# Second mixture of experts: gate and up from copied weights with H1 on the partitions, and gathers unspaced from the third half on

## The reference, cut to what matters

```python
# flat: 4096 x 128; gate_w, up_w: 32 x 128 x 128; down_w: 32 x 128 x 128
scores = softmax(flat @ router_w.T + router_bias)
topk_scores, topk_idx = top_k(scores, 4)
topk_scores /= topk_scores.sum(-1)
h = silu(flat x gate_w) * (flat x up_w)          # for each token and expert
expert_out = h x down_w
out = sum over the 4 chosen of expert_out * topk_score
out += silu(flat @ sgate_w.T) * (flat @ sup_w.T) @ sdown_w.T
x = layernorm(x + out)
```

## Time and profile before

| | us |
|---|---|
| median of 3 runs (lowest to highest) | 1296.8 (1296.16 to 1298.94) |
| time of the profiled execution | 1300.21 |
| its span in the profile | 1298.4 |
| TensorE busy | 1010.7 (78%) |
| VectorE busy | 811.9 (63%) |
| ScalarE busy | 547.4 (42%) |
| GpSimd busy | 489.5 (38%) |

### The profile page before, as it was taken

How to read it: one execution, slowest core, us unless ns; L and a number is a source line. 1 busy time by engine, 2 the same in 40 slices (tenths; PEclk the granted TensorE clock), 3 DMA queues, 4 the chain that set the end, 5 groups by cost and what they waited for, 6 DMA issues and landing times. The chain is left out here.

```text
span 1298.4 us, 20321 instructions
## 1 busy us (share of the span) xinstructions
PE 1010.7 (78%) x6768; PEld 602.2 (46%) x6768; DVE 811.9 (63%) x2127; ACT 547.4 (42%) x878; POOL 489.5 (38%) x484
## 2 busy tenths in 40 slices
PE   5772119952589899989989998988788989997971
PEld 3662016741234344434434443443247878874541
DVE  3757860132677788787887878688727443555643
ACT  1341004422136556665556665464464433431241
POOL 4101145525515410352004530143435544556776
PEclk8985558986569799997999999798899999999995
DMA  4225403421322211231122312353127756641122
GB/s 114 66 65 162 74 11 92 120 63 40 103 74 55 76 33 46 47 107 40 41 60 53 101 49 78 84 142 135 46 78 209 216 165 170 174 124 39 45 76 65
DMA packets 113122, 114.88 MB, mean 88 GB/s; under 512 B 17813, under 2 KB 95253, under 8 KB 109781
## 3 DMA queue, kind: packets, MB, share of 16 engines
q1 hardware_dynamic: 73830, 74.07, 20.7%
q0 software_dynamic: 12048, 25.71, 7.2%
q10 hardware_dynamic: 27144, 13.83, 3.7%
HBM read 67.94 MB, written 41.94 MB: 85 GB/s over the span
## 5 line engine op out<-in xcount | busy, mean ns | idle before, releaser
L2158 DVE TENSOR_REDUCE maxima<-psum 128x1 f32<-128x512 f32 (+4 forms) x624 | 385.5, 643 | 109.7 <-PE psum L1973 57.3
L2096 ACT ACTIVATE probs<-psum 128x1024 f32<-128x1024 f32 (+3 forms) x384 | 299.2, 809 | 271.9 <-PE psum L1992 206.4
L2006 PE MATMUL psum<-probs,v_wide 128*32 128x512 f32 (+3 forms) x1536 | 175.9, 532 | 0.0
L1969 PE MATMUL psum<-ka,qa 75*128 75x512 bf16 (+3 forms) x440 | 145.7, 344 | 28.4 <-DVE maxima L2158 22.8
L1481 POOL DMA_INDIRECT sorted<-x_rows,to_row x76 | 75.5, 993 | 209.3 <-ACT probs L2096 114.0
L2517 ACT ACTIVATE g_silu<-psum 128x512 f32<-128x512 f32 x80 | 47.8, 598 | 177.3 <-PE psum L2423 101.0
L1988 PE MATMUL psum<-qa,ka 78*128 78x512 bf16 (+3 forms) x440 | 118.4, 334 | 4.7 <-DMA qa<-max_parts 2.4
L1407 POOL DMA_INDIRECT w_gu<-expert_out,to_row x64 | 65.4, 1022 | 136.8 <-ACT probs L2096 95.3
L1969 PEld LDWEIGHTS psum<-ka,qa 75*128 75x128 bf16 x440 | 42.9, 99 | 129.5 <-DVE maxima L2158 111.0
L2423 PE MATMUL psum<-w_gu,g_xT 128*128 x384 | 95.4, 391 | 9.1 <-DVE g_h L2593 5.4
L116 POOL DMA_INDIRECT f_got<-expert_out,dense x64 | 63.9, 998 | 68.2 <-DMA f_got<-expert_out,dense 43.7
(11 more groups left out here) (333 smaller groups left out, 1825.7 us busy)
## 6 DMA issues: line engine op xcount, KB each, us to landing
g_rows<-sorted SPq DMA_DIRECT2D x192, 64.0 KB
expert_out<-g_y ACTq DMA_DIRECT2D x48, 256.0 KB
qa<-q_steps SPq DMA_DIRECT2D x30, 192.0 KB
ka<-k_steps SPq DMA_DIRECT2D x10, 576.0 KB
w<-in_W SPq DMA_DIRECT2D x16, 256.0 KB, 3.1
w_gu<-in_gu SPq DMA_DIRECT2D x4, 1024.0 KB, 10.7
sorted<-blank SPq DMA_DIRECT2D x54, 64.0 KB
q_steps<-w_gu SPq DMA_DIRECT2D x12, 256.0 KB
```

Source lines behind the costliest of these rows:

```text
L1969: mm = pe.matmul(bank[:, h * width:h * width + plain], qa[b][0:ROWS_MAX, h0 + h, qt * P:(qt + 1) * P], ka[b][0:ROWS_MAX, h0 + h, seg * HAL ...
L2006: mm = pe.matmul(B[OUT][32 * h:32 * (h + 1), q0 - c * HALF:HALF], v_wide[s.buf][:, j, h, PAD * (1 - c):PAD * (1 - c) + 32], probs[k % PRIN ...
L2096: act.activation(probs[k % PRING][:, 2 * pair:2 * pair + 2, 0:w], PS[:, 2 * pair:2 * pair + 2, 0:w], ACT.Exp).then_inc(exps, 1)
L2158: dve.tensor_reduce(maxima[:, seg, h0:h0 + heads, qt], bank[:, 0:heads * width].rearrange("p (h k) -> p h k", h=heads), AX.X, ALU.max).the ...
```

## The change

It does five things.

1. **Gate and up.** The operands change places. The expert's weights are stationary, once the gate half and once the up half, and xT streams past, 128 columns per tile. The result has H1 on the partitions and tokens along the free dimension, gate in one PSUM bank (two in turn) and up in another. The product h is already what the down product needs, so emit_hT and copy_hT go.
2. **Weights.** ScalarE copies each group's four [gate | up] blocks (128x256) from w_gu to one of two buffers w_now, at addresses from registers; it reads the expert numbers for two groups at even n. TensorE still reads them for the down product.
3. **Order.** The down product, the output copy and the store come one group sooner (n-1, n-1, n-2). On ScalarE the weight copies of n+1 stand between the store and SiLU n.
4. **Gathers.** PACED_HALVES is 2, so halves 2 and 3 are unspaced.
5. **Sums.** Their places in the two tables move.

```diff
-PACED_HALVES = 4
-SUMS_BESIDE_GROUPS = {31: (0, 0), 35: (0, 1), 38: (1, 0), 41: (1, 1), 45: (2, 0)}
-SUMS_BESIDE_CHUNKS = {(0, 1): (2, 1), (1, 0): (3, 0), (2, 0): (3, 1), (2, 3): (4, 0),
+PACED_HALVES = 2
+SUMS_BESIDE_GROUPS = {32: (0, 0), 36: (0, 1), 40: (1, 0), 44: (1, 1)}
+SUMS_BESIDE_CHUNKS = {(0, 0): (2, 0), (0, 3): (2, 1), (1, 2): (3, 0), (2, 1): (3, 1), (3, 0): (4, 0),
...
             if m < GROUPS:
-                return GU[:, :, 0, :], GU[:, :, 1, :]
+                return B[1 + 2 * (m % 2)], B[2]
...
                 def emit_group(n):
                     pe.wait_ge(xT_done, n + 1)
-                    wait_past(pe, h_done, n)
-                    for s in range(FT):
-                        at = (s % 2) * 2 * H1
-                        mm = pe.matmul(B[1 + s // 2][:, at:at + 2 * H1], xT[n % 2][:, s * P:(s + 1) * P],
-                                       w_gu[:, bass.ds(experts[n][s] * (2 * H1), 2 * H1)], start=(s % 2 == 0), stop=True,
-                                       skip_group_check=True)
-                    mm.then_inc(gu_psum, 1)
+                    pe.wait_ge(w_copied, n + 1)
+                    for x, (bank, filled) in enumerate(zip(gate_up(n), (gate_psum, gu_psum))):
+                        if x:
+                            wait_past(pe, h_done, n)
+                        for s in range(FT):
+                            mm = pe.matmul(bank[:, s * P:(s + 1) * P], w_now[n % 2][:, s, x * H1:(x + 1) * H1],
+                                           xT[n % 2][:, s * P:(s + 1) * P], start=(s == 0), stop=True, skip_group_check=True)
+                        mm.then_inc(filled, 1)
...
                     if n in PART_ENDS:
-                        emit_y(n - 2)
-                        emit_hT(n)
                         emit_y(n - 1)
                         emit_y(n)
                     if n + 1 < GROUPS:
                         emit_xT(n + 1)
-                    if n >= 2 and not within_end(n):
-                        emit_y(n - 2)
+                    if n and not within_end(n):
+                        emit_y(n - 1)
...
+                def copy_weights(n):
+                    if n % 2 == 0:
+                        load_experts(n)
+                    wait_past(act, gu_psum, n - 1)
+                    for s in range(FT):
+                        last = act.activation(w_now[n % 2][:, s, :], w_gu[:, bass.ds(experts[n][s] * (2 * H1), 2 * H1)], ACT.Copy)
+                    last.then_inc(w_copied, 1)
...
+                act.wait_ge(G.experts_loaded, 5 * 16)
+                copy_weights(0)
                 copy_xT(0)
                 for n in range(GROUPS):
-                    if n >= 3 and n - 3 not in range(PART_GROUPS - 3, PART_GROUPS):
-                        store(n - 3)
+                    if n >= 2 and n - 2 not in range(PART_GROUPS - 2, PART_GROUPS):
+                        store(n - 2)
                     if n == 1:
                         emit_scale(act, S, 1, LAST, x_last, 0, TB // 2)
+                    if n + 1 < GROUPS and n not in PART_ENDS:
+                        copy_weights(n + 1)
                     emit_silu(n)
-                    if n and n - 1 not in PART_ENDS:
-                        copy_hT(n - 1)
                     if n in PART_ENDS:
-                        copy_hT(n)
-                        for m in range(n - 2, n + 1):
+                        for m in range(n - 1, n + 1):
                             store(m)
                     if n == EXP_AT:
                         emit_exp1(act, S, LAST)
+                    if n in PART_ENDS:
+                        copy_weights(n + 1)
                     if n + 1 < GROUPS:
                         copy_xT(n + 1)
...
                 def emit_h(n):
-                    split = lambda x: x[:].rearrange("p (s h) -> p s h", s=FT)
+                    dve.wait_ge(gu_psum, n + 1)
                     dve.wait_ge(silu_done, n + 1)
-                    wait_past(dve, hT_psum, n - 1)
-                    dve.tensor_tensor(split(h[n % 2]), gate_up(n)[1], split(silu[n % 2]), ALU.mult).then_inc(h_done, 1)
+                    wait_past(dve, y_psum, n - 1)
+                    dve.tensor_tensor(hT[n % 2][:], gate_up(n)[1], silu[n % 2][:], ALU.mult).then_inc(h_done, 1)
```

More of the change, by code:

```diff
@@ L2295, in stage_experts1 @@
         rows = [M.sb(f"g_rows{v}", [P, FT, C]) for v in range(RING)]
-        xT, silu, h, hT = [[M.sb(f"{name}{u}", [P, HALF]) for u in two] for name in ("g_xT", "g_silu", "g_h", "g_hT")]
+        xT, silu, hT = [[M.sb(f"{name}{u}", [P, HALF]) for u in two] for name in ("g_xT", "g_silu", "g_hT")]
+        w_now = [M.sb(f"g_w{u}", [P, FT, 2 * H1]) for u in two]
+        w_copied = M.sem("w_copied")
         y = [M.sb(f"g_y{v}", [P, FT, C]) for v in range(RING)]
@@ L2328, in within_end @@
         def within_end(n):
-            return any(n - m in (0, 1, 2) for m in PART_ENDS)
+            return any(n - m in (0, 1) for m in PART_ENDS)
         def wait_kept(engine, n):
@@ L2419, in emit_group, with emit_y @@
                     pe.wait_ge(xT_done, n + 1)
-                    wait_past(pe, h_done, n)
-                    for s in range(FT):
-                        at = (s % 2) * 2 * H1
-                        mm = pe.matmul(B[1 + s // 2][:, at:at + 2 * H1], xT[n % 2][:, s * P:(s + 1) * P],
-                                       w_gu[:, bass.ds(experts[n][s] * (2 * H1), 2 * H1)], start=(s % 2 == 0), stop=True,
-                                       skip_group_check=True)
-                    mm.then_inc(gu_psum, 1)
-                def emit_hT(n):
-                    pe.wait_ge(h_done, n + 1)
[L2430 to L2436, removed]
+                    pe.wait_ge(w_copied, n + 1)
[6 more added lines that the diff above has]
+                        mm.then_inc(filled, 1)
+                def emit_y(n):
+                    pe.wait_ge(h_done, n + 1)
                     wait_past(pe, y_done, n)
@@ L2507, in _, with load_experts @@
             def _(act):
+                experts = {}
+                def load_experts(n):
+                    part, g = divmod(n, PART_GROUPS)
+                    act.wait_ge(table_read, part + 1)
+                    _, values = nc.values_load_multi_w_load_instructions(
+                        tile_tab[0:1, part, g * FT:(g + 2) * FT], engines=(mybir.EngineType.Activation,),
+                        min_val=0, max_val=E1 - 1, skip_runtime_bounds_check_because=
+                        "the tables count experts up from 0 and take the minimum with E1 - 1")
+                    experts[n], experts[n + 1] = values[:FT], values[FT:]
+                def copy_weights(n):
[5 more added lines that the diff above has]
+                    last.then_inc(w_copied, 1)
                 def copy_xT(n):
@@ L2513, in emit_silu @@
                 def emit_silu(m):
-                    act.wait_ge(gu_psum, m + 1)
+                    if m < GROUPS:
+                        act.wait_ge(gate_psum, m + 1)
+                    else:
+                        act.wait_ge(gu_psum, m + 1)
                     wait_past(act, h_done, m - 1)
-                    to = silu[m % 2][:]
-                    act.activation(to.rearrange("p (s h) -> p s h", s=FT) if m < GROUPS else to,
-                                   gate_up(m)[0], ACT.Silu).then_inc(silu_done, 1)
+                    act.activation(silu[m % 2][:], gate_up(m)[0], ACT.Silu).then_inc(silu_done, 1)
                 def store(n):
@@ L2566, in _ @@
                         emit_clear_end(act, G, S, ends[(e - SP_CLEARS) % 5])
-                copy_hT(GROUPS - 1)
-                store(GROUPS - 3)
                 for i in range(HALVES):
@@ L2698, in _ @@
                 queue.drain()
-                emit_y(GROUPS - 2)
                 for i in range(HALVES):
```

13 lines of the change are left out of this document (2 added, 11 removed).

## The result

The changed kernel takes 1310.6 us (median of 17 runs) where the kernel before, measured beside it, takes 1296.9 (17 runs): a ratio of 1.0082, 95% interval 1.006 to 1.0105. It is slower by 0.8%. (The ratios here are estimated over all runs of both kernels and can differ from the quotient of the medians, which is 1.0105 here, by up to 0.4%.) The forecast was a small gain, 1292.5 us; the time lies outside its range as well.

The account below looks back on a forecast made before the run. The prediction took the first part's end and GpSimd's gathers after it to bound the kernel. Gathers -18.1, later group 23 +16.2, shorter part end -2.4 gave -4.3 us: 1292.5 us against the median of 1296.8, range 1280 to 1308.

Parts of the forecast that it names:

- The loop on ScalarE and VectorE: Closed loop through output copy, store, weight copies and SiLU: 3.64 us, 4.24 with the register read, mean period 3.94.
- TensorE per group: TensorE's work in an expert group: 3.56 us instead of 3.74, with gate and up at 2.08.
- The part's end and the gathers: First part's end 2.4 us shorter, first gather at 1084.0; then gathers of halves three and four take 41.6 instead of 59.7.
- In time by 3.3: Second part's outputs stored at 1185.6, before GpSimd wants them at 1188.9.
- a gap before the 65th gather that waits for a store of outputs: On GpSimd's timeline: a sign that would show the prediction wrong.
- it waits for gathered rows before that too, up to 20 in all by my estimate; so it ends about where it does, while GpSimd still issues: Shared expert behind the second part: starts 16 us later, but waits of up to 20 leave its end about unchanged.
- the 18.1 of the gathers: On GpSimd: unspacing 32 gathers of halves three and four saves 18.1 us, all on the path.
- one wait of 8.03: Wait before the shared expert's last product, which starts at 1267.56; counted within waits of up to 20 in all.
- The read did not cost more: Rival: ScalarE's register read between store and weight copies costs 1.3 us, giving 1305.6 us; chance 0.30.
- TensorE did not set the pace: Rival: copies and reads hide, period 3.56, giving 1272.2 us; chance 0.14 for this or a half-way case at 1286.
- third rival: Free gathers of the third and fourth half stay at 1.87 because DMA is shared: 1310.6 us; chance 0.11.
- The Trainium skill's price for register reads: For ScalarE's read of 8 expert numbers: 1.6 us; by it the sum would be about 19 us longer.

Follow-up runs that it names:

- copies_first: The changed kernel with ScalarE's weight copies put ahead of the store in its order; ratio to the kernel before 0.9835.
- read_early: The changed kernel with ScalarE's register read moved behind the xT copy of the group before; ratio to the kernel before 0.9993.
- bank_after: The changed kernel with the shared expert's last down product in another PSUM bank, the experts' output bank; ratio to the kernel before 1.0033.
- gathers_only: The kernel before with only the gathers of halves 2 and 3 unspaced; ratio to the kernel before 0.9967.
- free_first: The changed kernel with weight copies ahead of the store, the last down product in another PSUM bank and no gather spaced; 1269.2 us, ratio 0.9812.

## Why the prediction was wrong

Point by point, by its own steps.

**The loop on ScalarE and VectorE: right in kind, a little short.** 3.64 and 4.24 were forecast, 3.72 and 4.37 came. The store issue with what follows it took 0.50, not 0.37; the copies 1.24, not 1.30; the read 0.55 (forecast 0.60) and 0.10 around it. The mean of 4.04 instead of 3.94 makes 2.4 on 23 groups: group 23 started 112.6 after group 0, where 110.2 was forecast. copies_first and read_early show that this loop, and nothing in TensorE, set the pace.

**TensorE per group: 3.56 was too high.** It is 3.17 when never starved. Its base was too large: 1.04 for eight passes of 128 columns, taken from one start to the next, held 0.15 that the passes themselves don't need, and 2.08 for sixteen doubled it. In copies_first they take 0.89 and 1.85. Where the 0.15 came from is not shown; the kernel before had no gap there either. It did not matter for the changed kernel, but it hid how much the order costs: 4.04 - 3.17 = 0.87 us a group, not 3.94 - 3.56 = 0.38.

**The part's end and the gathers: right in sum, in part by luck.** The first gather came 9.65 after group 23 (forecast 9.56), but with group 23 it stands 122.3 after group 0 where 119.8 was forecast. From there the errors cancel: the first two halves took 59.7 (63.3), the next two 43.5 (41.6), the last four to the last gather 92.2 (93.4). +2.5 - 3.6 + 1.9 - 1.2 = -0.4. So the last gather came at 1282.49 (1282.3 by the forecast's sum), 4.1 earlier than before. In the 43.5 is a wait of 2.05 for the second part's outputs. "In time by 3.3" was wrong, since group 47 started at 1179.15 and not at 1174.6, and a gap before the 65th gather that waits for a store of outputs is one of the signs of being wrong that the prediction had named.

**The step that failed** is "it waits for gathered rows before that too, up to 20 in all by my estimate; so it ends about where it does, while GpSimd still issues". Two numbers were wrong in it. The shared expert started 20.1 later, not 16: 18.6 from the first part, -0.8 from the part's end, 4.8 from the second part, -2.5 from the shorter tail of group 47. And its slack was not 20. From its start to the end the kernel before has 137.0, while the kernels that end by it, the last product in its old bank, have 123 to 125: **13 us of slack**. 9.7 of this lay ahead of its last product (106.1 before, 96.5 after), and 4 behind it. 20.1 - 13 makes the +6.5 to +7 of the stage, and the 18.1 of the gathers do not appear at all, because after 13 us they are no longer what ends last. Already with the forecast's own 16 the step would have given about +3 and not -4.3. I had read one wait of 8.03 and supposed twelve more; of that 8.03, 4.70 stays even when the gathers are early, since the product waits for VectorE's sum of the half before, and that follows the SiLU product of the last chunk (bank_after takes it away). The wait was only in part a wait for gathered rows.

**The rivals.** None came true. The read did not cost more, TensorE did not set the pace, the free gathers did gain their time. The time of 1310.6 coincides with that of the third rival, by another mechanism: its sign, the third half's gathers 1.6 apart or more, is absent. A fourth rival was missing: the engine behind the groups becomes the bound.

**The Trainium skill's price for register reads** ("Runtime: NRT & Kernel Launch", section Instruction fetch mechanics, about 200 ns per register, an estimate of 1.6 us for eight) was weighed and set aside; 0.55 for eight and 0.31 for four on ScalarE, 0.07 to 0.08 a register, bear that out.

## What to carry to other kernels

When a path is shortened by x and another piece of work is moved later by y, the gain ends at the distance between the two chains; measure the slack of the moved work as a time from its start to the end, down to what it depends on, and don't take a wait before its last step for slack until you know which engine ends that wait when the first cause is gone. Work added to an in-order engine should stand ahead of its waits: the same weight copies and reads cost 0.87 us a group behind the store's wait, and nothing that shows ahead of it.

## What was unexpected of the hardware

- **Clock after a pause.** The last product of 32 passes took 6.51 after 4.70 of waiting, and 3.84 after 1.41 (bank_after). The granted clock in these two stretches (windows of the changed kernel, TensorE alone, then of bank_after, all engines) is 0.57 and 1.00:

```profile
1278.54:1285.05 6.51, 6.51 (x32) 0.57 0.36 93
```

```profile
1272.39:1276.23 3.84, 3.84 (x32) 3.65 (x32) 3.67 (x13) 2.29 (x6) 2.92 (x4) 1.00 0.49 129
```

  The second is at the 2.4 GHz level; the first is at the 1.2 GHz level (0.50) up to 1283.5 and rises in the last 1.5 us. Ahead of the pause the clock was 1.00, in it 0.88 on average. So 2.7 us of the product's 6.51 came from the lower clock. After the same pause of 4.70, gathers_only's last product ran at 0.69 and took 5.44. The same shows at the head of the second part, in group 24's gate and up of the changed kernel behind its wait of 3.29; this is where the periods over 5 us came from:

```profile
1086.23:1089.90 3.67, 3.67 (x18) 0.54 0.14 40
```

- **Gathers let go beside the groups** cost the groups nothing that shows: in free_first they come 1.30 apart while the periods stay at 3.18, with TensorE, ScalarE and VectorE all at work.
- **Copies from SBUF to SBUF on ScalarE**, 128x256 in float32, follow each other 0.31 apart (1.33 for four), the same as the nearest row had it.
